# A two-layer feature-crossing tower: second layer by units of 32 rows in four column groups

## The reference, cut to what matters

```python
for W in (W0, W1):                      # W0: 1024 x 128, W1: 4096 x 128
    prev = x.shape[1]                   # 32, then 128
    z = einsum('bhd,bmd->bhmd', e, x).reshape(b, 32 * prev, 32)
    x = einsum('bpd,pj->bjd', z, W)
    res.append(x)
z = sum(concatenate(res, axis=1), axis=-1)          # 256 a row
h = relu(concatenate([z, dense_ctx], 1) @ W_top1 + b_top1)   # 272 -> 512
h = relu(h @ W_top2 + b_top2)                                # 512 -> 256
y = h @ W_top3
```

## Time and profile before

| | |
|---|---|
| median of 3 runs | 377.0 us (376.52 to 378.28) |
| the profiled execution | 377.42 us |
| its span, first to last instruction | 375.6 us |
| PE / PEld busy | 87% / 82% |
| DVE / ACT / POOL busy | 55% / 61% / 67% |
| second layer's matmuls, L741 | 864 records, 107.4 us |
| triples, L698 | 512 records, 76.3 us |
| gathers, L280 | 256, 251.7 us busy |

### The profile page before, as it was taken

One profiled execution on the slowest core, in us unless ns is written; L12 is line 12 of the kernel. 1 busy time (PEld: TensorE's weight loads), 2 busy tenths in 40 slices (PEclk: granted clock), 3 DMA queues, 4 the chain that ended last, 5 costly groups with the idle time before them and its releaser, 6 DMA issues.

```text
span 375.6 us, 11527 instructions
## 1 busy us (share of the span) xinstructions
PE 327.3 (87%) x4646; PEld 307.0 (82%) x4646; DVE 205.2 (55%) x869; ACT 229.9 (61%) x774; POOL 252.4 (67%) x262
## 2 busy tenths in 40 slices
PE   2989957278999899899989998999799888999897
PEld 1777746167999899899979998999798877999797
DVE  4336999932666466646655655556555453555201
ACT  2578566077667666766676667766765565666601
POOL 5777887877777777777777777777777777740000
PEclk9999985569999999999999999999999999999999
DMA  7801000000010101001001111010101010100000
GB/s 218 315 14 16 9 11 15 11 14 14 16 18 14 16 15 15 17 17 16 14 16 15 17 15 18 14 17 15 16 14 16 14 17 15 16 12 2 3 0 2
DMA packets 10774, 9.79 MB, mean 26 GB/s; under 512 B 4665, under 2 KB 8897, under 8 KB 10721
## 3 DMA queue, kind: packets, MB, share of 16 engines
q0 software_dynamic: 8192, 4.21, 7.6%
q1 hardware_dynamic: 2528, 4.84, 3.8%
HBM read 9.03 MB, written 0.00 MB: 24 GB/s over the span
## 4 chain that ended last, share of the span: by engine, by line
POOL 66%; issue 21%; PE 8%; ACT 2%; DMA 1%; POOLq 0%; DVE 0%; SPq 0%
POOL emb L280 66%; PE WA L741 3%; ACT TS L287 1%; PE M L754 1%; DMA emb<-in_table,rows 1%; DMA base<-in_bases 1%; PE M L773 1%; PE M L764 0%; ACT eblk L287 0%; POOLq L83 0%; ACT h L361 0%; PE PA L698 0%; PE QB L708 0%; PE T L802 0%; PE M L765 0%
## 5 line engine op out<-in xcount | busy, mean ns | idle before, releaser
L280 POOL DMA_INDIRECT emb<-in_table,rows x256 | 251.7, 983 | 80.4 <-issue 77.7
L741 PE MATMUL WA<-TS,RX 128*128 128x128 f32 x864 | 107.4, 277 | 1.0 <-ACT TS L287 1.0
L741 PEld LDWEIGHTS WA<-TS,RX 128*128 128x128 f32 x864 | 101.0, 192 | 1.8 <-issue 1.2
L591 DVE COPY TS<-T 32x48 f32<-32x48 f32 x256 | 51.1, 200 | 78.1 <-PE T L725 71.1
L287 ACT ACTIVATE eblk<-ET 32x256 f32<-32x256 f32 x128 | 48.6, 380 | 54.1 <-PE ET L685 51.8
L698 PE MATMUL PA<-eblk,zP 128*128 128x132 f32 x512 | 76.3, 285 | 1.9 <-ACT TS L287 1.1
L558 DVE TENSOR_TENSOR zQ<-ET,eT 128x1024 f32<-128x1024 f32 x32 | 39.2, 1224 | 61.5 <-ACT eT L287 61.5
L698 PEld LDWEIGHTS PA<-eblk,zP 128*128 128x128 f32 x512 | 67.9, 198 | 2.7 <-ACT TS L287 1.5
L287 ACT ACTIVATE TS<-T 32x48 f32<-32x48 f32 (+1 forms) x320 | 62.8, 196 | 7.8
L552 DVE TENSOR_TENSOR zP<-ET,eT 128x224 f32<-128x224 f32 (+6 forms) x224 | 47.6, 287 | 0.0
L287 ACT ACTIVATE TS<-PA 128x396 f32<-128x396 f32 (+1 forms) x96 | 44.5, 463 | 3.4 <-PE PA L698 2.3
(11 more groups left out here) (90 smaller groups left out, 320.3 us busy)
## 6 DMA issues: line engine op xcount, KB each, us to landing
emb<-in_table,rows POOLq DMA_INDIRECT x256, 2.4
TS<-in_W SPq DMA_DIRECT2D x8, 256.0 KB, 5.4
wt<-in_W_top SPq DMA_DIRECT2D x2, 512.0 KB, 8.6
y1w<-in_W_rows SPq DMA_DIRECT2D x1, 448.0 KB, 7.0
TS<-in_W_rows SPq DMA_DIRECT2D x1, 448.0 KB, 8.0
sym<-in_W_cols SPq DMA_DIRECT2D x1, 264.0 KB, 2.8
TS<-in_W_cols SPq DMA_DIRECT2D x1, 264.0 KB, 3.1
idc<-in_ids SPq DMA_DIRECT2D x1, 128.0 KB, 2.1
```

The lines of the kernel that those rows point to most:

```text
L280: eng.indirect_dma_start(emb[par][:, g, :], None, table, bass.IndirectOffsetOnAxis(rows[:, k, g:g + 1], 0))\
L591: eng.tensor_copy(view(ts[32 * q:32 * q + 32, :, :], P * REST + b0, [[P, 6], [1, 8]]), view(src, 1 + q, [[NQ, 6], [C25, 8]])).then_inc(t3_ ...
L741: m = eng.matmul(WA[:, 0:P], C[:, kt, :], TS[k % 2][:, slot_of(kt), :], start=(kt == 0), stop=(kt == KT - 1))
```

## The change

- **Second layer by units.** For each unit, 54 + 7 matmuls take 32 rows of `TS` as weights (32 columns) and stream the 128 columns of `C` or `y1w`. Matmul number x goes to column group x mod 4, so that four lie side by side and four partial sums stand below one another in WA (columns 0 to 255). ACT copies them to `S`, and `folded` adds the four parts and turns them, by two matmuls against a stack of four 32 x 32 identities. After a tile's fourth unit ACT copies both halves to `zf`.
- **When.** The second layer of unit 0 stands in unit 7, in three pieces (32, 16 and 13 matmuls) ahead of the first and second trio and between across and other triples. Units 8, 11, 14, 17, 21 and 25 hold two units' second layers, so that unit 31 holds that of unit 30; the last is in `last_tile`. The tower's three steps stand at trio 2 of one unit and trios 0 and 2 of the next.
- **Transposes at the unit's own beginning** rather than a unit ahead; ACT makes `eT` first and `eblk` from it; DVE starts after `eT`, with the products of the triples first. Units 0 and 1 are transposed after steps 12 and 22.
- **Weights turned in unit 6** (banks 0 to 3, 4 to 8, 9 to 13 after its three trios); DVE copies the odd banks.
- **Early copies on ScalarE.** For units 0 to 5 ACT makes all 20 copies of T3. DVE's `late_sums` are five parts instead of three.

The diff, cut to its core:

```diff
+        START = 7
+        TWICE = (8, 11, 14, 17, 21, 25)
+        PIECES = (range(0, F), range(F, F + HALF), range(F + HALF, KT + Y1T))
-        EARLY_AT = (8, 18)
+        EARLY_AT = (12, 22)
+        ALONE = 6
...
 # ACT, eblk_copy(u)
+                copy(eT[:, :], ET[:, 0:GROUPS * F]).then_inc(et_kept, 1)
+                eng.wait_ge(et_kept, u + 1)
                 for v in range(NQ):
...
-                    copy(dst, ET[r, 0:GROUPS * F].rearrange("p (g x h) -> p g x h", x=2, h=HALF)).then_inc(eblk_made, 1)
-                copy(eT[:, :], ET[:, 0:GROUPS * F]).then_inc(eblk_made, 1)
+                    copy(dst, eT[r, :].rearrange("p (g x h) -> p g x h", x=2, h=HALF)).then_inc(eblk_made, 1)
...
 # ACT, trio r of unit u
+                    if r == 0 and piece is not None and piece[1][-1] == KT + Y1T - 1:
+                        s_copy(piece[0])
+                    part_copy(t)
+                    if r == 2 and piece is not None:
+                        s_copy(piece[0])
+                    if r < 2 and u > 0:
+                        if u - 1 < ALONE:
+                            rest_copies(u - 1, r)
+                        rest_copies(u - 1, r + 2)
+                    if C_AT <= t < C_END:
+                        for q in range(C_TO[t - C_AT], C_TO[t - C_AT + 1]):
+                            if q % 2 == 0:
+                                c_copy(q)
...
 # DVE
+            for u in range(OWN, ALL):
+                products(u, 0)
+                products(u, 1)
+                if u > ALONE:
                     for part in range(3):
                         rest_copies(u - 1, part)
+                products(u, 2)
+                if u - OWN < 4:
+                    late_sums(u - OWN + 1)
+                if u == C_AT // TRIOS:
+                    for q in range(1, CB, 2):
+                        c_copy(q)
...
 # PE
+            def second(u, pieces):
...
+                for n in pieces:
+                    if n < KT:
+                        x, count, slot, w, c0 = n, KT, slot_of(n), C[:, n, :], 0
+                    else:
+                        x, count, slot, w, c0 = n - KT, Y1T, Y1_SLOTS[n - KT], y1w[:, n - KT, :], P
+                    j = x % NQ
+                    m = eng.matmul(WA[32 * j:32 * j + 32, c0:c0 + P], TS[k % 2][:, slot, 32 * unit:32 * unit + 32], w,
+                                   start=(x < NQ), stop=(x + NQ >= count))
+            def folded(u):
...
+                eng.wait_ge(s_kept, u + 1)
+                for c in range(2):
+                    m = eng.matmul(WA[:, 2 * P + P * c + 32 * unit:2 * P + P * c + 32 * unit + 32], S[:, P * (1 - c):P * (2 - c)], istack,
+                                   start=True, stop=True)
...
+            for u in range(ALL):
+                if u >= OWN:
+                    emb_transposes(u)
+                for r in range(TRIOS):
+                    t = TRIOS * u + r
+                    if folded_at(u, r) is not None:
+                        folded(folded_at(u, r))
+                    if r == 0 and u in L2_AT:
+                        hidden2(L2_AT[u])
+                    if r == 2 and u in L1_AT:
+                        hidden1(L1_AT[u])
+                    if r == 2 and u in L2_AT:
+                        result(L2_AT[u])
+                    if r < TRIOS - 1 and second_at(u, r) is not None:
+                        second(*second_at(u, r))
+                    triples(t)
+                    if r == TRIOS - 1:
+                        across_triples(u)
+                        if second_at(u, r) is not None:
+                            second(*second_at(u, r))
+                        other_triples(u)
+                    if C_AT <= t < C_END:
+                        for q in range(C_TO[t - C_AT], C_TO[t - C_AT + 1]):
+                            weights(q)
 # last_tile
+                folded(ALL - 2)
+                second(ALL - 1, range(KT + Y1T))
...
+                folded(ALL - 1)
+                eng.wait_ge(zf_kept, TILES)
```

More of the change, by code:

```diff
@@ L383, in _ @@
                     eblk_copy(EARLY_AT.index(h))
+            for j in range(NQ):
+                copy(istack[32 * j:32 * j + 32, :], ident[32 * j:32 * j + 32, 32 * j:32 * j + 32]).then_inc(stack_made, 1)
             eng.wait_ge(tower_loaded, 16 * 5)
             copy(wt3[:, :, 0], vec[:, N1 + N2:]).then_inc(wt3_made, 1)
[L386 to L408, removed]
@@ L555, in products @@
                 if part == 0:
-                    eng.wait_ge(eblk_made, (NQ + 1) * (u + 1))
+                    eng.wait_ge(et_kept, u + 1)
                     wait(eng, t3_made, u - 1)
[L558 to L562, removed]
-                        apart(s)
-                if part == 2:
-                    for s in range(5, SUB):
+                    for s in range(1, SUB):
                         apart(s)
@@ L581, in rest_copies @@
                 eng.wait_ge(t3_made, u + 1)
-                if unit == 0 and part == 0:
-                    wait(eng, y2_made, k - 1)
-                    wait(eng, y1_made, k - 1)
+                if part == 0:
+                    wait(eng, s_made, u - 2 * UNITS + 1)
                 for j, q in itertools.product(range(2), range(NQ + 1)):
@@ L815, in _ @@
                     emb_transposes(EARLY_AT.index(h))
-            for t in range(TOTAL):
-                u, r = divmod(t, TRIOS)
-                if r == 0 and len(EARLY_AT) <= u + 1 < ALL:
-                    emb_transposes(u + 1)
-                triples(t)
-                if r == TRIOS - 1:
-                    across_triples(u)
-                    other_triples(u)
-                if C_AT <= t < SLOTS_TILE:
-                    for q in range(C_TO[t - C_AT], C_TO[t - C_AT + 1]):
-                        weights(q)
-                if y2_range(t) is not None:
-                    second(*y2_range(t))
-                if tile_at(t, Y1_AT) is not None:
-                    first(tile_at(t, Y1_AT))
-                if tile_at(t, L1_AT) is not None:
-                    hidden1(tile_at(t, L1_AT))
-                if tile_at(t, L2_AT) is not None:
-                    hidden2(tile_at(t, L2_AT))
-                if tile_at(t, Y_AT) is not None:
-                    result(tile_at(t, Y_AT))
+            for u in range(ALL):
+                if u >= OWN:
+                    emb_transposes(u)
+                for r in range(TRIOS):
+                    t = TRIOS * u + r
+                    if folded_at(u, r) is not None:
+                        folded(folded_at(u, r))
+                    if r == 0 and u in L2_AT:
+                        hidden2(L2_AT[u])
+                    if r == 2 and u in L1_AT:
+                        hidden1(L1_AT[u])
+                    if r == 2 and u in L2_AT:
+                        result(L2_AT[u])
[10 more added lines that the diff above has]
+                            weights(q)
             last_tile()
```

190 lines of the change are left out of this document (110 added, 80 removed).

## The result

The changed kernel takes 428.72 us (median of four runs, 426.72 to 434.26), the kernel before 376.76 beside it: a ratio of 1.135, with an interval of 1.132 to 1.139; the slowest of the four, 1.8% above the fastest, is left out of the ratio. The forecast was 404 with a range of 380 to 414: slower was right, the size was not. The profiled execution took 426.72 with a span of 424.9, where the sum gave 402.8. So 22.1 us of span are missing.

A forecast was written before the change was run, and what follows sets the result against it. It took POOL's gathers, then PE's tail, to bound the kernel before, and PE the changed one: 112 + 275.5 + 15.3 = 402.8 us of span, plus 1.4, gives 404 us, 7% slower; range 380 to 414.

The forecast's parts named there:

- the sum: Whole span: 112 us up to unit 7, 275.5 for units 7 to 31, 15.3 after them; 402.8 us.
- Does it stall?: Units from 7 on: triples' wait for ACT and DVE, about 2.65 us after the transposes, just hidden by 2.76 of PE work.
- The front: Before unit 7: ACT's copy queue sets rounds of 10.0 us for units 2 to 5; unit 7 begins at 112 (97 to 121).
- Unit 6: Unit with the turning of 14 weight banks: 18.5 us, 24 at half clock, 12.6 if ACT's own work were all.
- A unit's price: PE's time for a single unit from unit 7 on: 4.00 + 3.57 + 0.70 + 0.42 = 8.69 us.
- A visit of four column groups: Rounds of four between full-array work: array division changes each way, 0.12 + 0.23 us, two visits a unit, 0.70.
- a unit's fold: Two matmuls a unit, 4 records priced like the transposes at 0.105 each: 0.42 us.
- a round: Four second-layer matmuls side by side: 0.111 to 0.131 us, taken as 0.1114; 32 a unit make 3.57 us.
- The tail: After unit 31's other_triples: copies, last second layer, fold, zf's copy and the end as before; 15.3 us.
- the gathers stay the clock (360): Rival: units 7 to 30 average under 9.98 us, last transposes again at 335.05, the tail shrinks; 360 us, chance 0.12.
- the front is early (388): Rival: ACT doesn't hold the front, unit 7 begins when its gathers land at 95.4; 388 us, chance 0.20.
- four groups don't run side by side at full rate (424): Rival: a second-layer round takes 0.131 us, adding 20 us; 424 us, chance 0.04.

The follow-up runs named there:

- the shared copies: Changed kernel with ALONE = 1 for 6, so that DVE makes ten of the twenty T3 copies from unit 1 on: 419.43 us (one run).
- the three edits: Changed kernel with zf's copy ahead of eblk's, T3 copies shared from unit 1, and weight-bank copies ahead of T3's: 403.66 us, ratio 1.070.

## Why the prediction was right in its direction and wrong in its size

- **"Does it stall?" is the step that failed.** It counted the wait of a unit's triples for eT, eblk and products, and found it just hidden; in units without a new tile it was (unit 9 above). It did not look at what `second` itself waits for. At a tile's first unit that is zf, behind eT and eblk on ACT, before any of the rounds that were to be the cover: 17.2 us in seven tiles, with about 4.2 us lost at half clock. In the sum this wait stood at nothing. Moving that one copy took 13.5 us back. The prediction had named the condition ("A PE clock below full after unit 7 would break every term") without an idea of what would bring it about.
- **The front**: unit 2's transposes came 1.6 us earlier than forecast (52.0), the rounds of units 2 to 5 were 10.5, 10.0, 9.6 and 10.4 us, forecast 10.0, and for the reason given, as the shared copies showed. **Unit 6** was mis-sized: 23.0 us against 18.5. The bound of 24 at half clock was in the text; the clock was the half one for most of it. PE and ACT in the kernel after:

```profile
97.28 2.14 ACT L331 ACTIVATE TS<-T 32x48 f32<-32x48 f32 x10
97.50 1.06 PE L741 MATMUL WA<-ident,RT 128*128 128x128 f32 x4
...
99.45 0.60 ACT L331 ACTIVATE RX<-M 128x512 f32<-128x512 f32 x1
...
100.10 1.12 PE L741 MATMUL M<-ident,RT 128*128 128x128 f32 x4 [1.54 <-ACT RX L331]
```

  A bank takes 1.06 us on PE instead of 0.60, and the copy behind ten T copies is there as forecast. I took the full-clock sum although showed the low clock exactly where PE was idle as here.
- **A unit's price** was right and a little high: single units without a wait 8.45 to 8.53 against 8.69, a double 12.44 against 12.68. A visit of four column groups costs about 0.34 us, forecast 0.35; a unit's fold 0.36 without the change behind it, forecast 0.42; a round 0.109, forecast 0.1114. Over the 24 units PE's busy time, without what the clock added, is some 5 us less than the forecast (265.8 - 4.2 against 266.8), which hid a part of the miss.
- **The tail** was right: 25.4 and 24.1 us against 24.0. The difference in the kernel after is the clock, half from 410.6 to 414.0; that began within this wait of 2.18 us:

```profile
411.27 4.47 PE L820 MATMUL WA<-RX,TS 128*32 128x128 f32 x106 [2.18 <-ACT TS L331]
```

- **The sum**: 3.5 + 17.3 + 1.4 = 22.2 us of span; the rest of the 24.7 to the median is that the profiled execution lies 2.0 below it, where 0.4 above was assumed.
- **The rivals.** That the gathers stay the clock (360) fell: they are done 67 us before PE needs the last. That the front is early (388) fell at 115. That four groups don't run side by side at full rate (424) gave the nearest time, by luck: a round of 128 columns in four groups takes 0.109 us, no more than a record in the whole array. The 2.38x (79% of three) that the Trainium skill ("TensorE: Matmul & The Clock Gate", "Measured speedup vs the span model") gives for three column groups, there with 512 columns, does not hold for these four.
- **Why the shorter tail doesn't pay.** Of the 40.55 us behind the last transposes before, PE was busy for 36.60:

```profile
335.05:375.60 40.55, 36.60 (x442) 35.30 (x442) 8.70 (x38) 16.35 (x62) 0.00 (x0) 1.00 0.01 2
```

  The tail was work, not latency. Doing it earlier pays only where PE is idle earlier, and of that there was little: 6.4 us of waits for gathers and 8.3 in the tower. The change takes some 15 us off the tail and pays for it with about 12 us of folds (32 x 0.36), 17 of visits (0.34, twice in 25 units), 3 of rounds (32 of 0.109 against 30.5 of 0.1114, in 32 units) and a second layer that starts 15 to 24 us later (106 to 115 instead of 91.64).

## What to carry to other kernels

Where a change moves a step, list every semaphore that the moved step waits for, and for each what is queued ahead of its releaser on that engine; the largest of these is the term, not the one of the operation that looks new. A dependent chain costs nothing only while PE has other work between its steps, so before you shorten a tail ask whether it is idle time or work: work has to go somewhere. And when you take work out, ask what it covered: half of the folds and one visit were worth less than their own duration here.

## What the runs showed of the hardware

- In the kernel after, four waits of PE, of 2.49, 2.70 and 2.49 us for zf and of 2.18 us in the tail, came with 3.4 us at half the granted clock, which began in the last 0.4 to 0.8 us of the wait. Three others of 2.49 to 2.50 us and one of 2.04 us had none. The same wait of 2.04 us had such a stretch in the kernels with the early zf copy and with the three edits. It costs 1.3 to 1.6 us more than the wait itself. What tells the two kinds apart is open.
- Four column groups with 128 streamed columns each run at the rate of one matmul in the whole array, 0.109 us a round; narrower weights save no time in this kernel, they only keep it. A visit of them between full-array matmuls costs 0.34 us (unit 9 above).
- A matmul with 128 weight columns and 32 streamed ones costs nearly as much as one with 128 streamed: the starts of a fold's four records in unit 9 lie 0.03, 0.11 and 0.11 us apart, full-array records with 132 streamed columns 0.112. With one of the two matmuls left out, a unit without a wait was 0.21 to 0.22 us shorter.

Open: a version in which only the folds, and not `second`, wait for zf was not tried, as PE would then write the tile WA while ACT reads it. The 6.1 us of zf waits that remain with the copy moved, most of it 0.67 us for the copies of eT and zf themselves and one of 2.0 us in unit 25, were not taken apart further.
